# A Mamba and mixture-of-experts block on one core: the third norm's turn, copy and routing product ahead of the sum over states of the unit behind

## The reference

```python
x = x + ref_attn(layernorm(x))      # a Mamba layer and a gated feed-forward
x = x + moe(layernorm(x))           # eight experts, the best two for each token

# ref_attn, with D_INNER 256, D_STATE 16, D_CONV 4:
u = ln(x, n1_g, n1_b); x_in, z = split(u @ in_proj_w.T)
xc = silu(conv4(x_in) + conv_b); dt, B, C = split(xc @ x_proj_w.T)
delta = softplus(dt @ dt_w.T + dt_b)
h_t = exp(delta_t * A) * h_{t-1} + delta_t * B_t * xc_t     # for each of 16 states n
y_t = sum_n h_t[n] * C_t[n] + D * xc_t
x = x + (y * silu(z)) @ out_w.T
gate, val = split(ln(x, n2_g, n2_b) @ ffg_w.T + ffg_b)
x = x + (silu(gate) * val) @ ffp_w.T + ffp_b

# moe, on the third norm of the result:
top_w, top_idx = top_k(x @ Ws + bs, 2); top_w = softmax(top_w)
out = sum over the two experts e of top_w * ((silu(x @ Wg[e]) * (x @ Wu[e])) @ Wd[e])
```

## Time and profile before

| | |
|---|---|
| median of three executions | 910.73 us (905.72 to 913.05) |
| the profiled execution | 908.7 us |
| its span, first to last instruction | 906.5 us |
| VectorE busy | 735.0 us (81%) |
| TensorE busy | 669.6 us (74%) |
| GpSimd busy | 575.0 us (63%) |
| ScalarE busy | 496.7 us (55%) |
| mean granted TensorE clock | 0.870 |

### The profile page before, as it was taken

The page is one execution under the profiler, slowest core; times in us unless marked ns, Lnnn a source line. Parts: engine busy times, 40 slices in busy tenths (PEclk is TensorE's granted clock), DMA queues, the critical chain, the costliest instruction groups (busy, mean ns, idle before and its releaser), DMA issues.

```text
span 906.5 us, 13029 instructions
## 1 busy us (share of the span) xinstructions
PE 669.6 (74%) x3684; PEld 487.7 (54%) x3684; DVE 735.0 (81%) x1135; ACT 496.7 (55%) x1070; POOL 575.0 (63%) x488
## 2 busy tenths in 40 slices
PE   4467578778767786797789778877885586888964
PEld 1144244445335544683477347734773375787963
DVE  1378879989998999979998999999999985453463
ACT  3447676766776576546745665657554442422421
POOL 1185556566756895799778976898579825335422
PEclk9669699799979987898799969988897788988997
DMA  7833133223312336532653355336543534447693
GB/s 180 242 116 108 47 96 114 84 64 112 119 39 93 100 112 187 160 112 97 192 148 107 99 173 158 118 88 182 154 130 112 167 100 125 132 126 200 183 309 112
DMA packets 96458, 120.07 MB, mean 132 GB/s; under 512 B 11463, under 2 KB 63507, under 8 KB 96371
## 3 DMA queue, kind: packets, MB, share of 16 engines
q1 hardware_dynamic: 91843, 109.86, 41.6%
q0 software_dynamic: 4544, 9.38, 2.8%
HBM read 107.20 MB, written 16.34 MB: 136 GB/s over the span
## 4 chain that ended last, share of the span: by engine, by line
PE 25%; DVE 20%; issue 12%; ACT 6%; DMA 2%; SPq 2%; another core or an unknown queue 1%; POOL 0%; DVEq 0%; ACTq 0%; POOLq 0%
DVE state L951 10%; PE gate L1250 3%; PE up L1268 2%; DVE product L961 2%; PE up L1257 2%; PE y L1156 2%; PE y L1151 2%; PE work_front L1107 2%; PE work_front L1113 1%; ACT decay L815 1%; DVE stats L881 1%; DVE silu_m L1072 1%; DVE x_tok L990 1%; PE decay L1250 1%
## 5 line engine op out<-in xcount | busy, mean ns | idle before, releaser
L696 POOL TENSOR_TENSOR inflow<-du,b_wide 128x1024 f32<-128x1024 f32 x128 | 317.3, 2482 | 177.5 <-DVE product L961 116.9
L951 DVE TENSOR_TENSOR_SCAN state<-decay,carry,inflow 128x512 f32<-128x512 f32 x192 | 235.1, 1266 | 4.2 <-ACT decay L815 4.0
L815 ACT ACTIVATE decay<-delta,a_neg 128x512 f32<-128x512 f32 x256 | 172.1, 690 | 113.6 <-DVE state L951 107.2
L961 DVE TENSOR_TENSOR product<-state,c_wide 128x1024 f32<-128x1024 f32 (+1 forms) x105 | 144.8, 1379 | 4.8 <-PE y L1151 3.4
L723 POOL DMA_INDIRECT y_dram<-y_rows,x_rows x78 | 87.6, 1123 | 93.5 <-ACT y_rows L871 86.3
L1151 PE MATMUL y<-ident,product 128*128 128x128 f32 x748 | 111.7, 294 | 42.5 <-DVE product L961 42.5
L1151 PEld LDWEIGHTS y<-ident,product 128*128 128x128 f32 x748 | 91.9, 152 | 80.4 <-DVE product L961 50.1
L1156 PE MATMUL y<-h_rows,ident 128*128 128x512 f32 x138 | 90.2, 773 | 28.5 <-ACT h_rows L780 28.5
L717 POOL DMA_INDIRECT row_dram<-m_tok,place x64 | 72.6, 1134 | 24.6 <-issue 14.6
L951 DVE TENSOR_TENSOR_SCAN state<-decay,inflow 128x512 f32<-128x512 f32 x64 | 74.7, 1211 | 9.6 <-ACT decay L815 7.0
L1107 PE MATMUL work_front<-u_t,w_tap 128*128 128x512 f32 x128 | 65.7, 641 | 6.0 <-ACT u_t L751 4.4
(11 more groups left out here) (210 smaller groups left out, 1274.4 us busy)
## 6 DMA issues: line engine op xcount, KB each, us to landing
b_wide<-bc_dram SPq DMA_DIRECT2D x128, 256.0 KB
c_wide<-bc_dram SPq DMA_DIRECT2D x105, 256.0 KB
w_stage<-gate_up_dram SPq DMA_DIRECT2D x78, 344.0 KB
x_rows<-row_dram SPq DMA_DIRECT2D x78, 65.0 KB
x_tok<-in_x SPq DMA_DIRECT2D x8, 256.0 KB, 5.9
out<-x_tok SPq DMA_DIRECT2D x8, 256.0 KB
inflow<-y_dram SPq DMA_DIRECT2D x6, 256.0 KB, 4.0
gate_up_dram<-in_Wg SPq DMA_DIRECT2D x1, 1376.0 KB, 9.2
```

Source lines behind the costliest of these rows:

```text
L696: e.tensor_tensor(inflow[:, key % 3], du[:, c % 2], b_wide[:, key % ROW_SLOTS:key % ROW_SLOTS + 1, :].to_broadcast([P, HALVES, CHUNK]), AL ...
L815: e.activation(decay_bank[h][:], delta[:, c % 2, h, :], ACT.Exp, scale=a_neg[:, h, n:n + 1]).then_inc(S["decay"], 1)
L951: e.tensor_tensor_scan(state[:, key % STATE_SLOTS, h, :], decay_bank[h][:], inflow[:, key % 3, h, :], 0.0 if c % (SEQ // CHUNK) == 0 else ...
L961: e.tensor_tensor(product[:, key % 2, :, :wide], state[:, key % STATE_SLOTS, :, :wide], c_wide[:, key % ROW_SLOTS:key % ROW_SLOTS + 1, :wi ...
```

## The change

Two rows of `BACK` move steps to their first part, and the first part of the `BACK` row goes ahead of `total` of the unit behind. For the other rows of `BACK` the first part is empty or on GpSimd, where there is no `total`; so only rows 6 and 12 get another order, each in seven chunks. The first part of the `FRONT` row stays behind `total`. In the tail nothing changes, since there the parts follow each other at once.

```diff
@@ BACK
-    (("n_turn",), ("n_t",), ("ff_gate",)),
+    (("n_turn", "n_t"), (), ("ff_gate",)),
     ((), ("gate_h",), ("ff_val",)),
     ((), ("silu_g", "ff_h"), ("ff_out",)),
     ((), ("x_four", "stats3"), ()),
     (("rstd3",), (), ()),
     ((), ("shift3",), ("m_tok",)),
-    (("m_turn",), ("m_t",), ("route_mm",)),
+    (("m_turn", "m_t", "route_mm"), (), ()),
@@ plan
         fetch("inflow", i + 2)
+        put_all(back[0])
         if i:
             put("total", i - 1)
-        put_all(back[0], front[0])
+        put_all(front[0])
         add()
```

## The result

The changed kernel takes 929.29 us (median of four executions: 921.85, 924.57, 934.01, 935.22), the kernel before, run beside it, 911.11 (four, 905.72 to 913.05). The ratio is **1.0228, 95% interval 1.0182 to 1.0273**: slower by 17 to 25 us, and 20.8 at the ratio itself (0.0228 x 911.1). The forecast was 11.2 us more. The four executions fall in two pairs, and the longer pair has the lower mean granted clock: 921.85 and 924.57 us at 0.858 and 0.857, 934.01 and 935.22 at 0.844 and 0.848.

What follows compares the result with a forecast made beforehand. VectorE's order of scans, products and expert steps was taken to set the pace. Losses of 6.8 + 3.0 + 1.4 = 11.2 us on the median of 910.7 gave 922 us, 1.2% slower, range 906 to 931.

Steps and rivals of the forecast that it cites:

- the 5.3 us: Waits of `logits` for the routing product, 3.4 us in chunk 1 and 1.9 in chunk 2; their removal was booked as nothing.
- The rivals on the other side: Whole kernel: delay hidden, 914 us, 22%; waits for `logits` go and nothing else appears, 905, 10%; waits swapped, 911, 8%.
- the rival of 929: Chunks 3 to 7, row 12: TensorE's clock falls in the chains too, another 6.5 us together, 929 us; 15%.
- I take the middle, 1.5 us: Row 12, chunks 1 and 2: `total` of unit 12 comes later, 1.5 us taken for each chunk, 3.0 together.
- Its lower case: Row 12, chunk 1: the chain from `m_tok` takes 7.1 us, so `total` of unit 12 starts 0.7 us later.
- its upper case: Row 12, chunk 1: the sum of unit 11 runs slow again after a pause 1.5 us longer, delay 2.2 us.
- the sum of the chain: Row 12, chunks 3 to 7: added durations from the start of `m_turn` until `silu_m` can start, 5.9 us.
- the forecast's 6.8 us: Row 12, chunks 3 to 7: VectorE stands still before `silu_m` for 0.6, 1.4, 1.6, 0.8 and 2.4 us.
- Row 6: 1.4 us, with 2.8 as its upper end: `n_t` ahead of `decay` of unit 7 delays the scan: 0.7 us in chunk 3, 0.5 in 1, 0.2 in 6.
- the other four: Row 6, chunks other than 1, 3 and 6: no loss, as the scan starts later than the delayed `decay` is ready.

## Why the prediction was right or wrong

- **The side and the places: right.** Slower, in row 12 of all chunks and in row 6, with the named steps waiting. `logits` waits for nothing, and the 5.3 us gained nothing, as booked. The rivals on the other side are out: `total` of unit 12 starts at 199.75 and 287.88, where 193.5 and 276.3 decided. (Part of this is that the execution was late there already; from the end of `m_tok` it is 10.7 us in both, against 6.4 and 4.9.)
- **The size: too small, 11.2 us where 17 to 25 were measured.** The median itself, 929.3, lies in the range, 906 to 931, and on the rival of 929, but neither for the forecast's reasons: the range was wide, and the rival put into chunks 3 to 7 alone what came there, in chunks 1 and 2 and in row 6. Three terms were too small.
- **"I take the middle, 1.5 us" in chunks 1 and 2 is the step that failed first.** Its lower case let the chain run at full clock; its upper case let only the sum of unit 11 run slow. In the run all that stands behind the pause is slow, the turn, the routing product, the sum and the turns of the state: 10.7 us and not 7.1, and so a loss of 4.3 and 3.2 us in the trace, 7.5 together for 3.0. Row 12 in these chunks alone measured 7.6. The row that warned of it was at hand: a sum at 3.51 us behind a pause of 1.66, where the change was to make the pause nearly twice as long. It didn't decide alone, since the same sum behind the same pause ran at full speed in chunk 2 of the same trace. With the clock held the chain is 6.8 us, so the rest of that sum was right to 0.3.
- **The clock in chunks 3 to 7 was a rival at 15%, and it held in four of five in the profiled execution,** which was the slowest; with row 12 alone it held in one of five. The reason given against it, that a wait of 0.57 us had left the clock high, said nothing of one of 1.45. On the other hand the sum of the chain was 0.6 too long: 5.9 estimated, 5.28 at full clock. So the forecast's 6.8 us became 8.5, where full clock would have given 3.5. The two errors hid each other, and that this term came out near is luck.
- **Row 6: 1.4 us, with 2.8 as its upper end, was sized wrong.** Alone it measured 4.5 us (1.4 to 7.7), and more without the turn ahead of the sum. Two steps of the term failed. The scan of unit 7 was to wait in chunks 1, 3 and 6 and in "the other four" not at all; it waits in chunks 2 and 5 as well, 3.4 us in all with row 6 alone and 4.9 in the changed kernel, and only chunk 3 came out near (0.7 forecast, 0.51 and 0.92 measured). And it was left out who shares a port with VectorE. I read ScalarE's and TensorE's rows and not GpSimd's, in which a duration of 3.33 us beside a usual 2.36 would have shown that `product` and `inflow` meet there and VectorE wins by 0.12 us.
- **Still open.** Chunks 1 and 2 with 3 to 7 make 2.2%, row 12 at once 1.6%. Single executions differ: in the traces of the nine kernels that leave row 6 alone, this stretch differs from the kernel before by -2.8 to +2.3 us, probably as the pairs of VectorE and GpSimd fall one way or the other. So a loss under 3 us in one trace stands here only where the timing agrees. What makes the clock fall behind a pause of 1.45 us in four chunks and not in a fifth, and behind one of 1.66 or 2.15 us at one place and not at another, was not settled. Nor was it tried to change the port sharing by itself, so the price of the port is read from the pairs of rows alone, and that of row 6 from the waits, these pairs and the turn that cost nothing measurable.

## What to carry to other kernels

A step that is put first in an in-order queue brings its wait with it. Count what work covered that wait where it stood, and then count everything behind it a second time at the lower clock, if the engine is TensorE and the trace shows the low clock behind a pause as short as the new one, be it at one place only. Count all the places where the moved step stands, not only the one whose timeline you read. Before moving anything that delays the bounding engine by a fraction of a microsecond, look at which of its instructions run beside an engine that shares its ports, and by how little they come first. And if a result is needed earlier, look for the gap in which its engine idles already, before putting it in front of other work.

## What the runs showed of the hardware

- Float32 matmuls behind a pause of 3.18 or 3.19 us ran at 1.2 GHz (granted clock 0.50) in every case shown here: four transposes 1.11 or 1.12 us in place of 0.60 to 0.66, eight routing instructions 1.87 in place of 1.06, four of 128x512 3.62 to 3.76 in place of 1.96. Behind 1.45 us the turn itself still took 0.66 in chunks 4 and 5; the steps after the second pause, of 0.69, were slow in one (0.53) and at full speed in the other (1.00). Pauses of 1.66 and of 2.14 or 2.15 us were followed by either: 3.51 or 1.98 us for one sum, 1.87 or 1.06 for one routing product.
- Useless matmuls in a wait were worth 8.7 us of 20.8 in the changed kernel, where the pause was bare, and cost 2.6 (0.2 to 5.1) in the kernel before, where the wait was 0.57 us. With the turns alone moved they brought nothing measurable.
- VectorE instructions that start 0.16 to 0.89 us behind a GpSimd one, both reading two operands from SBUF, lost 1.3 to 2.1 us (`product` 1.24 to 2.54, 2.95 and 3.02, `gate_h` 0.67 to 2.65 and 2.74). They end at a fixed distance from the end of the GpSimd instruction, 1.08 to 1.09 us for `product` and 0.54 to 0.55 for `gate_h`. The other way round GpSimd lost 1.0 (2.35 to 3.33) and VectorE nothing.
